# Openings of the first and third attention rearranged: barrier ahead of the gate loads, queries of the first 512 tokens between key units, normalisation on ScalarE, rows of maxima sent ahead of the last queries

## The chip, the cores and the metric

The kernel runs on one core of a Trainium2 chip as one program for the five engines of the core: PE (TensorE), DVE (VectorE), ACT (ScalarE), POOL (GpSimd) and SP (SyncE, which issues most of the DMAs). The metric is the device time of one execution in microseconds (us). Three executions of the kernel before were timed; the profile is of a fourth.

## What is computed

Four transformer layers over x, 2048 tokens of width 256. Each layer is cross attention over a context of 1601 rows of width 192, then a layer of experts (FFN); both add to x.

```
x = x + L0_xattn(layernorm(x), ctx)      # 16 heads of 16
x = x + L0_ffn(layernorm(x))             # 16 experts, top 4, and a shared one
x = x + L1_xattn(...); x = x + L1_ffn(...)   # 16 heads; 8 experts, top 2
x = x + L2_xattn(...); x = x + L2_ffn(...)   # 8 heads of 32; 8 experts, top 2
x = x + L3_xattn(...); x = x + L3_ffn(...)   # 16 heads, masked; 16 experts, top 2

def xattn(x, y):
    q = x @ Wq + bq; k = y @ Wk + bk; v = y @ Wv + bv      # split into heads
    att = softmax(q @ k.T * dh ** -0.5)                    # over the 1601 keys
    return (att @ v) @ Wo + bo
```

## The kernel before

Tokens stand in four chunks of 512 (`NQ = 4`, `Q = 512`), heads in four groups (`NG = 4`; 4 heads a group in layers 0, 1 and 3, 2 in layer 2), keys in 13 blocks of up to 128 (`NK = 13`). An attention loops over chunks (`iteration`), in a chunk over groups, in a group over the 13 key blocks: PE makes scores, ACT takes exp, PE weighs the values.

Queries and keys are held as three bf16 parts each. Such a "unit" (128 rows of queries or keys by 512 columns) goes through a pipeline with two buffers (`QK[2]`, `QP[2]`, dealt in turn by the class `Staging`; whoever fills a buffer waits until the unit before last has been split and has landed): PE projects it into PSUM, ACT copies it out twice (`copy_keys`, lines 1115 and 1116; first queries line 1150), DVE or POOL splits it into parts (`split`), SP stores it in DRAM (`store_key_parts` into `k_parts`, line 514; `store_query_parts` into `q_parts`, line 523) and loads it back stacked (`load_keys` into `k_stack`, line 457, six DMAs a group; `load_queries` into `q_stack`, lines 541, 546 and 547, seven DMAs a group). All 256 columns of keys need eight key units: units 0 to 3 hold the first two groups of heads, units 4 to 7 the other two. A chunk of queries is two units, m = 0 and 1.

The largest score of each token and head is needed before exp. It is found with 400-column "max" jobs: a matmul into one of three PSUM banks (line 2193) and a reduce on DVE (line 1458). When all of a group's jobs are through, the maxima are turned on PE, negated and split on DVE into `m_part`, and SP sends them through DRAM into the query stack (`store_max_rows`, lines 583 and 588). The scores of the group can't start before that.

Attentions 1 and 3 (`AHEAD`) have their opening hidden in the FFN ahead. Attentions 0 and 2 have an opening of their own, the prologue: the max jobs of group 0 (64 in layer 0, 32 in layer 2), the turn, and three eighths of the jobs of group 1 (24 and 12). Between them, after every second job, PE takes one item of the list `behind`: in layer 0 key units 4 to 7 (two halves each) and the 13 value blocks (lines 2109 and 2110), 21 items, and then in both layers for chunks d = 1, 2, 3 two items "turn" (the normalised chunk transposed, `turn_ahead`, line 2258) and four items "query" (`query_ahead`, line 2271). ACT copies those queries once (line 1190), and POOL makes the first part as well as the split (`split_queries`, line 874).

The very start: SP issues x's first chunk, the context and the attention weights, then x's other three chunks, the mask and the gate weights, and then comes a barrier of all five engines (`fence`); only behind it PE, ACT and DVE begin. Key units 0 to 3 run first, then DVE's statistics of x, the normalisation of chunk 0 (DVE) and of chunks 1 to 3 (POOL, line 839), and the two query units of chunk 0.

In layer 2 keys and values are projected in the FFN ahead; what is left for its opening are the statistics of x, the loads, values and queries.

In both openings SP's queue stands in one written order. In layer 0 it is: key units 0 to 3, all six loads of groups 0 and 1, the first queries, key units 4 to 7, the loads of groups 2 and 3, the rows of maxima, then the queries of chunks 1 to 3. In layer 2: the loads of group 0, the first queries, the loads of groups 1 to 3, the queries of chunks 1 to 3, then the rows of maxima.

## Time and profile before

| | |
|---|---|
| three timed runs | 3899.71, 3901.49, 3909.51 us; median 3901.49 |
| the profiled execution | 3903.35 us, span of its instructions 3901.6 us |
| busy in the span | PE 3615.8 us (93%), DVE 2534.6, ACT 1913.4, POOL 682.8 |
| granted clock of TensorE, mean | 0.964 of full speed |

Spans and starts below are microseconds from the first instruction. A busy share says that an instruction was under way, and idle time of an engine that nobody waits for costs nothing, so the two openings are read stretch by stretch, by what ended each wait.

### The profile page before, as it was taken

To read this page: it belongs to the slowest core of one execution; us is meant where nothing else is said; L and a number is where in the kernel's file an instruction comes from. 1 tells how busy PE (TensorE), PEld (TensorE's weight loads), DVE (VectorE), ACT (ScalarE), POOL (GpSimd) and SP (SyncE) were. 2 spreads that over 40 slices of the span, in tenths; PEclk is the share of its full clock that TensorE was granted. 3 is DMA by queue.
4 is the path that set the end of the run, shared out by engine and by line. 5 is a ranking of instruction groups with operands and counts; after the bars stand their busy time and mean duration, and the time that the engine had idled before them with its cause. 6 is when DMAs were issued, how large, how long until landed. Compare 5 with 4: busy or idle time off the path is not lost. (4 is left out here: it accounts for less than half of the span.)

```text
span 3901.6 us, 50396 instructions
## 1 busy us (share of the span) xinstructions
PE 3615.8 (93%) x17554; PEld 1565.4 (40%) x17555; DVE 2534.6 (65%) x5369; ACT 1913.4 (49%) x2321; POOL 682.8 (17%) x976
## 2 busy tenths in 40 slices
PE   5999999789999999987998699999789999998996
PEld 2333333355543333334665333333433333333564
DVE  4888888446678888844223555554468888885523
ACT  2677777511137777772332244445202777777111
POOL 3300001300032000013221401010403100001142
PEclk8999999889999999998999899999899999999998
DMA  6200000151000000006001500000420000001134
GB/s 133 48 19 14 18 17 7 54 100 42 21 23 27 14 19 18 10 20 242 31 30 46 118 18 18 18 18 6 87 63 21 27 13 19 18 10 43 48 124 137
DMA packets 132652, 171.33 MB, mean 44 GB/s; under 512 B 38378, under 2 KB 106588, under 8 KB 130256
## 3 DMA queue, kind: packets, MB, share of 16 engines
q1 hardware_dynamic: 122288, 142.42, 12.8%
q0 software_dynamic: 10144, 26.08, 3.4%
q8 instruction: 126, 2.06, 0.2%
q14 instruction: 94, 0.77, 0.1%
HBM read 131.27 MB, written 40.84 MB: 44 GB/s over the span
## 5 line engine op out<-in xcount | busy, mean ns | idle before, releaser
L1458 DVE TENSOR_REDUCE mx<-ps 128x1 f32<-128x400 f32 (+1 forms) x3584 | 1819.6, 567 | 500.4 <-PE ps L2193 488.6
L1206 ACT ACTIVATE probs<-ps,zero_col 128x1024 f32<-128x1024 f32 (+1 forms) x1040 | 1111.1, 1111 | 585.0 <-PE ps L2229 584.8
L2193 PE MATMUL ps<-k_stack,q_stack 97*128 97x400 bf16 (+1 forms) x3584 | 1074.5, 338 | 53.4 <-DMA q_stack<-m_parts 21.6
L2229 PE MATMUL ps<-q_stack,k_stack 100*128 100x512 bf16 (+2 forms) x3328 | 1056.3, 381 | 6.4 <-ACT probs L1206 6.4
L2243 PE MATMUL ps<-probs,v 128*32 128x512 f32 (+2 forms) x5824 | 890.8, 607 | 0.2 <-ACT probs L1206 0.2
L2193 PEld LDWEIGHTS ps<-k_stack,q_stack 97*128 97x128 bf16 x3584 | 289.8, 97 | 1049.8 <-DVE mx L1458 624.9
L1206 ACT ACTIVATE probs<-ps,mask_col 128x1024 f32<-128x1024 f32 (+1 forms) x416 | 439.5, 1110 | 158.6 <-PE ps L2229 158.6
L2229 PEld LDWEIGHTS ps<-q_stack,k_stack 100*128 100x128 bf16 (+2 forms) x3328 | 323.2, 100 | 345.0 <-ACT probs L1206 65.8
L2243 PEld LDWEIGHTS ps<-probs,v 128*32 128x32 f32 (+2 forms) x5824 | 140.0, 111 | 263.9 <-issue 248.6
L1611 DVE SCALAR_TENSOR_TENSOR x_res<-ps,comb,x_res 128x256 f32<-128x256 f32 x336 | 148.5, 480 | 87.0 <-PE ps L2485 81.9
L1274 ACT ACTIVATE h_t_s<-ps 128x512 f32<-128x512 f32 x80 | 47.8, 597 | 278.2 <-PE ps L2476 278.2
L2485 PE MATMUL ps<-w_up_s,h_t_s 128*128 128x256 f32 x640 | 166.7, 391 | 6.8 <-DVE x_res L1611 3.5
L2476 PE MATMUL ps<-xn_t,w_up_s 128*128 128x512 f32 x320 | 154.2, 605 | 18.7 <-DMA w_up_s<-in_expert 18.1
L922 POOL TENSOR_TENSOR o_t<-o_sum,recip_wide 128x512 f32<-128x512 f32 x32 | 40.8, 1274 | 711.6 <-DMA recip_wide<-row_recips 711.6
L924 POOL TENSOR_TENSOR o_sum<-o_sum,recip_wide 128x512 f32<-128x512 f32 x28 | 35.8, 1277 | 647.2 <-DMA recip_wide<-row_recips 647.2
L2566 PE MATMUL ps<-w_all,xn_t 128*128 x624 | 142.8, 382 | 3.7 <-ACT xn_t L1288 2.4
L2545 PE MATMUL ps<-w_all,xn_t 128*128 x312 | 143.3, 603 | 1.8 <-SPq L769 1.8
L2485 PEld LDWEIGHTS ps<-w_up_s,h_t_s 128*128 128x128 f32 x640 | 116.3, 192 | 60.1 <-DVE x_res L1611 26.4
L2566 PEld LDWEIGHTS ps<-w_all,xn_t 128*128 128x128 f32 x624 | 117.1, 190 | 42.0 <-issue 27.9
L1288 ACT ACTIVATE xn_t<-ps,tile_bias 128x128 f32<-128x128 f32 x312 | 84.7, 382 | 99.8 <-PE ps L2557 99.5
L2499 PE MATMUL ps<-w_up_s,xn_t 128*128 128x512 f32 x256 | 121.6, 618 | 11.0 <-DMA w_up_s<-in_we 10.4
L1318 ACT ACTIVATE silu_gate<-ps 128x320 f32<-128x320 f32 (+3 forms) x60 | 28.1, 468 | 195.5 <-PE ps L2641 152.0
(291 smaller groups left out, 2727.3 us busy)
## 6 DMA issues: line engine op xcount, KB each, us to landing
q_stack<-q_parts SPq DMA_DIRECT2D x384, 64.0 KB, 2.3
q_parts<-qk_part SPq DMA_DIRECT2D x32, 384.0 KB, 2.5
w_up<-in_up SPq DMA_DIRECT2D x17, 704.0 KB, 4.1
w_up_s<-in_expert SPq DMA_DIRECT2D x40, 256.0 KB, 2.7
k_stack<-k_parts SPq DMA_DIRECT2D x48, 200.1 KB, 8.1
k_stack<-k_parts POOLq DMA_DIRECT2D x48, 200.1 KB, 18.6
k_parts<-qk_part SPq DMA_DIRECT2D x24, 384.0 KB, 3.1
w_all<-in_up SPq DMA_DIRECT2D x8, 1024.0 KB, 15.3
```

Source lines behind the costliest of these rows:

```text
L1206: act.activation(PR[pair[0] % 4][0:r, :, :], PS[0:r, 2 * b:2 * b + 2, :], ACT.Exp, bias=mask_col[0:r, k:k + 1] if L == 3 else zero_col[0:r ...
L1288: last = act.activation(HB[:, q * P:(q + 1) * P], PS[:, 2 + q // 4, q % 4 * P:(q % 4 + 1) * P], ACT.Gelu, bias=BT[:, bass.ds(i, 1), q], sc ...
L1458: ins = dve.reduce_max(MX4[g % 2][:, u, c:c + 1], PS[:, bank, 0:CK[c]], AX.X)
L1611: dve.scalar_tensor_tensor(X[:, t, :], PS[:, b, 0:D], c, X[:, t, :], ALU.mult, ALU.add).then_inc(s_yf, 1)
L2193: last = mm(PS[:, bank, 0:CK[c]], QS[g][0:97, slot_of(j), qt * P:(qt + 1) * P], KS[0:97, (g * hpg + j) * nsub, CKO[c]:CKO[c] + CK[c]], sta ...
L2229: last = mm(PS[0:r, b + i, :], KS[0:rows, (g * hpg + jj) * nsub + sub, k * P:k * P + r], QS[g][0:rows, slot_of(jj) + sub, :], start=sub == ...
L2243: last = mm(PS[pw * jj:pw * jj + pw, 4, :], V[0:r, k, (g * hpg + jj) * pw:(g * hpg + jj) * pw + pw], PR[used[0] % 4][0:r, i, :], start=k = ...
L2476: last = mm(PS[:, n % 2, :], up[:, k, :], xnT[:, k, c * Q:(c + 1) * Q], start=k == 0, stop=k == 1)
L2485: mm(PS[:, 2 + yj[0] % 3, 0:D], HTS[n % 2][:, 0, i * P:(i + 1) * P], weight_slot(load)[1], start=True, stop=True).then_inc(s_y, 1)
L2499: last = mm(PS[:, n % 4, :], xnT[:, k, t * P:(t + 1) * P], WUS[i % 2][:, k * 512:(k + 1) * 512], start=k == 0, stop=k == 1)
L2545: last = mm(PS[:, half, :], XT1[par][:, k * P:(k + 1) * P], w1.rearrange("p a f -> p (a f)"), start=k == 0, stop=k == 1)
L2566: last = mm(PS[:, 4 + par, 0:D], HB[:, q * P:(q + 1) * P], w2.rearrange("p a f -> p (a f)"), start=q == 0, stop=q == NF // P - 1)
```

## The change

First attention (layer 0):
- The barrier stands directly behind the issue of the attention weights. The issue of x's chunks 1 to 3 comes after it on SP; the mask and the gate weights (nine DMAs) are issued by ACT ahead of its own part of the barrier.
- The units run in the order key 0, key 1, key 2, query (0,0), key 3, query (0,1) (`FIRST_UNITS`). Statistics and normalisation of chunk 0 come before them on DVE, those of chunks 1 to 3 after them.
- SP stores units 0 to 2, query (0,0) and key 3, waits for all to land, and loads queries of group 0, keys of group 0, queries of group 1, keys of group 1; only then does it store query (0,1).
- Values 4 to 12 are projected after the queries of chunks 1, 2 and 3 (`LATE_VALUES`), all through one PSUM bank, number 4.

Both openings:
- ACT instead of POOL normalises chunks 1 to 3 (`normalize_ahead`, 12 activations of 128x256, with `shift` = -mean/deviation as the bias), behind the load of the Exp table.
- ACT writes both copies of the queries of chunks 1 to 3; POOL's first copy goes.
- SP sends the rows of maxima after the queries of chunks 1 and 2 and before those of chunk 3; the keys of groups 2 and 3 are loaded last.

In layer 2 the loads of group 0 are cut in two: rows 0 and 1 ahead of the store of query (0,0), the other four behind it.

```diff
     if L == 0:
-        return keys[0:4] if part == 0 else [x for pair in zip(keys[4:8], values[0:4]) for x in pair] + values[4:]
+        return [x for pair in zip(keys[4:8], values[0:4]) for x in pair]
...
+FIRST_UNITS = ["key", "key", "key", "query", "key", "query"]
+LATE_VALUES = {1: range(4, 7), 2: range(7, 10), 3: range(10, NK)}
+
+def value_bank(L, v):
+    return 4 if L == 0 and v >= 4 else 2 + v % 2
...
             load_attention_weights(0)
+            fence(sp, fences)
             for c in range(1, NQ):
                 sp.dma_start(X[:, c * TPQ:(c + 1) * TPQ, :], x_chunks[c]).then_inc(s_in, 16)
-            sp.dma_start(mask_u8[:, 0:NK - 1], A["mask"][:, 0:P * (NK - 1)].rearrange("a (k p) -> p (a k)", p=P),
...
-            fence(sp, fences)
             load_constant_rows(0)
-            for u in range(4):
+            for u in range(3):
                 store_key_parts(u)
+            store_query_parts(0, 0)
+            store_key_parts(3)
+            wait_landed(qd)
             wait_landed(kd)
+            load_queries(0, (0, 0), 0)
             load_keys(sp, 0, 0)
+            load_queries(0, (0, 1), 1)
             load_keys(sp, 0, 1)
+            store_query_parts(0, 1)
+            wait_landed(qd)
+            load_queries(0, (0, 2), 2)
 
             def first_queries(L):
                 store_query_parts(0, 0)
+                if L == 2:
+                    load_keys(sp, 2, 0, (2, 6))
                 wait_landed(qd)
...
-                if L not in AHEAD:
-                    first_queries(L)
                 if L == 2:
-                    for g in range(1, NG):
-                        load_keys(sp, 2, g)
+                    first_queries(2)
+                    load_keys(sp, 2, 1)
                 if L == 0:
                     for u in range(4, 8):
                         store_key_parts(u)
                     wait_landed(kd)
-                    load_keys(sp, 0, 2)
-                    load_keys(sp, 0, 3)
-                    store_max_rows(L, 0)
                 if L not in AHEAD:
-                    for d in range(1, NQ):
+                    for d in range(1, NQ - 1):
                         for m in range(2):
                             store_query_parts(d, m)
-                if L == 2:
                     store_max_rows(L, 0)
+                    for m in range(2):
+                        store_query_parts(NQ - 1, m)
+                    for g in range(2, NG):
+                        load_keys(sp, L, g)
...
                 pool.wait_ge(s_qe, qe.at())
-                link(pool.tensor_copy(QP[buf][:, 0, :], QK[buf][:]))
+                if L in AHEAD:
+                    link(pool.tensor_copy(QP[buf][:, 0, :], QK[buf][:]))
                 split(QK[buf], QP[buf], Q, s_qp)
...
-                    for d in range(1, NQ):
-                        normalize_chunk(d, XNQ[d])
...
+            def normalize_ahead():
+                act.wait_ge(s_rs, rs.at())
+                for d in range(1, NQ):
+                    for i in range(TPQ):
+                        t = d * TPQ + i
+                        last = act.activation(XNQ[d][:, i, :], X[:, t, :], ACT.Identity,
+                                              bias=shift[:, t:t + 1], scale=rstd[:, t:t + 1])
+                    last.then_inc(s_xp, 1)
...
                 act.activation(warm[:], zero_col[:], ACT.Exp)
+                if L not in AHEAD:
+                    normalize_ahead()
                 if L == 0:
                     copy_projections(0, 1)
...
                 if not fresh:
-                    pe.wait_ge(s_vc, vc.at(1))
+                    pe.wait_ge(s_vc, vc.at(0 if L == 0 and v >= 4 else 1))
...
                     behind += [("query", (d, m, k)) for m in range(2) for k in range(2)]
+                    behind += [("value", n) for n in LATE_VALUES[d]] if L == 0 else []
```

On SP's queue the start of the program, from the issue of x's later chunks up to the first send of the rows of maxima, stood as follows before (the loads of mask and gates and the constant rows, which come in between, and the seven-DMA query loads are part of it).

```order
L597 DMA x_res<-in_x 128x4x256 x3
...
L514 DMA k_parts<-qk_part 128x3x512 x3
L514 DMA k_parts<-qk_part 128x3x65
L457 DMA k_stack<-k_parts 16x4x1601 x12
L523 DMA q_parts<-qk_part 128x3x512
L541 DMA q_stack<-q_parts 16x4x512 x6
...
L514 DMA k_parts<-qk_part 128x3x512 x3
L514 DMA k_parts<-qk_part 128x3x65
L457 DMA k_stack<-k_parts 16x4x1601 x12
L583 DMA m_parts<-m_part 16x4x128
L588 DMA q_stack<-m_parts 4x2048
L523 DMA q_parts<-qk_part 128x3x512 x6
```

The same queue of the changed kernel, from the key units to the last keys.

```order
L524 DMA k_parts<-qk_part 128x3x512 x3
L533 DMA q_parts<-qk_part 128x3x512
L524 DMA k_parts<-qk_part 128x3x65
L551 DMA q_stack<-q_parts 16x4x512 x6
...
L467 DMA k_stack<-k_parts 16x4x1601 x6
L551 DMA q_stack<-q_parts 16x4x512 x6
...
L467 DMA k_stack<-k_parts 16x4x1601 x6
L533 DMA q_parts<-qk_part 128x3x512
...
L533 DMA q_parts<-qk_part 128x3x512 x4
L593 DMA m_parts<-m_part 16x4x128
L598 DMA q_stack<-m_parts 4x2048
L533 DMA q_parts<-qk_part 128x3x512 x2
L467 DMA k_stack<-k_parts 16x4x1601 x12
```

The first query store moved in front of all key loads, the second one behind the loads of both groups, the maxima in front of the last two query stores, and twelve key loads behind those.

On PE, in the prologue of layer 0, the last key half (65 columns) was followed before by ten value blocks with two max jobs between each two.

```order
L2094 MATMUL ps<-ctx_b,wk 128x65
L2193 MATMUL ps<-k_stack,q_stack 128x400 x2
L2109 MATMUL ps<-wv,ctx_a 128x256
L2110 MATMUL ps<-wv,ctx_b 128x256
L2193 MATMUL ps<-k_stack,q_stack 128x401
L2193 MATMUL ps<-k_stack,q_stack 128x400
L2109 MATMUL ps<-wv,ctx_a 128x256
L2110 MATMUL ps<-wv,ctx_b 128x256
```

In the changed kernel one value block (number 3) follows it and then the first transposes of chunk 1.

```order
L2153 MATMUL ps<-ctx_b,wk 128x65
L2255 MATMUL ps<-k_stack,q_stack 128x400 x2
L2168 MATMUL ps<-wv,ctx_a 128x256
L2169 MATMUL ps<-wv,ctx_b 128x256
L2255 MATMUL ps<-k_stack,q_stack 128x401
L2255 MATMUL ps<-k_stack,q_stack 128x400
L2320 MATMUL ps<-ident,probs 128x128 x4
```

The transposes, which wait for ACT's copy of key unit 7 (`pe.wait_ge(s_kc, kc.at())` in `turn_ahead`), moved from item 22 of `behind` to item 13.

On SP's queue in the opening of layer 2, behind the last loads of the FFN, there stood before:

```order
L503 DMA k_stack<-const_rows 1x16x1601 x4
L457 DMA k_stack<-k_parts 32x2x1601 x6
L523 DMA q_parts<-qk_part 128x3x512
L546 DMA q_stack<-q_parts 32x2x512 x6
...
L523 DMA q_parts<-qk_part 128x3x512
L546 DMA q_stack<-q_parts 32x2x512 x6
...
L457 DMA k_stack<-k_parts 32x2x1601 x18
L523 DMA q_parts<-qk_part 128x3x512 x6
L583 DMA m_parts<-m_part 8x4x128
L588 DMA q_stack<-m_parts 4x2x512
```

and in the changed kernel:

```order
L513 DMA k_stack<-const_rows 1x16x1601 x4
L467 DMA k_stack<-k_parts 32x2x1601 x2
L533 DMA q_parts<-qk_part 128x3x512
L467 DMA k_stack<-k_parts 32x2x1601 x4
...
L467 DMA k_stack<-k_parts 32x2x1601 x6
L533 DMA q_parts<-qk_part 128x3x512 x4
L593 DMA m_parts<-m_part 8x4x128
L598 DMA q_stack<-m_parts 4x2x512
L533 DMA q_parts<-qk_part 128x3x512 x2
L467 DMA k_stack<-k_parts 32x2x1601 x12
```

Of the six query stores ahead of the rows of maxima two moved behind them, and with them the keys of groups 2 and 3.

## Rows read from the trace of the kernel before

**Rows 1.** The page, section 1: busy us, share, instructions of each engine.

```profile
PE 3615.8 (93%) x17554; PEld 1565.4 (40%) x17555; DVE 2534.6 (65%) x5369; ACT 1913.4 (49%) x2321; POOL 682.8 (17%) x976
```

**Rows 2.** Windows: stretch, length, busy PE, PEld, DVE, ACT, POOL, clock, DMA share, GB/s.

```profile
28.50:64.20 35.70, 7.97 (x16) 3.95 (x16) 16.29 (x54) 6.84 (x14) 15.44 (x12) 0.60 0.73 123
64.20:73.50 9.30, 9.27 (x18) 4.56 (x19) 4.23 (x8) 1.53 (x4) 2.91 (x3) 0.50 0.40 123
82.95:123.80 40.85, 35.92 (x150) 19.39 (x150) 34.25 (x71) 11.70 (x32) 16.46 (x21) 0.97 0.63 108
...
2174.50:2202.00 27.50, 23.94 (x93) 10.95 (x93) 22.61 (x49) 6.71 (x12) 14.78 (x15) 1.00 0.82 185
2202.00:2223.50 21.50, 0.02 (x1) 0.06 (x2) 0.96 (x2) 1.37 (x2) 18.29 (x23) 0.53 0.30 101
```

**Rows 3.** Timeline of SP's queue, first opening: start, length, instruction.

```profile
7.16 0.35 SPq L494 DMA_DIRECT2D bo<-in_bo  x1
...
10.72 1.35 SPq L598 DMA_DIRECT2D mask_u<-in_mask  x1
...
26.50 7.79 SPq L514 DMA_DIRECT2D k_parts<-qk_part  x4
37.22 5.49 SPq L457 DMA_DIRECT2D k_stack<-k_parts  x12
...
52.37 0.38 SPq L523 DMA_DIRECT2D q_parts<-qk_part  x1
...
59.40 2.65 SPq L541 DMA_DIRECT2D q_stack<-q_parts  x6
...
73.50 10.91 SPq L514 DMA_DIRECT2D k_parts<-qk_part  x4
```

**Rows 4.** Timeline of DVE and ACT, first opening; in brackets the idle time before.

```profile
19.46 1.41 DVE L1434 BATCH_NORM_STATS2 stat<-x_res 128x6 f32<-128x256 f32 x4 [19.33 <-SPq L436]
30.28 0.60 ACT L1115 ACTIVATE qk<-ps 128x512 f32<-128x512 f32 x1 [2.93 <-DMA k_parts<-qk_part]
...
82.59 0.23 ACT L1115 ACTIVATE qk<-ps 128x65 f32<-128x65 f32 x1 [2.36 <-DMA k_parts<-qk_part]
```

**Rows 5.** Windows, for DMA: the start, and two stretches full of key loads.

```profile
2.00:28.00 26.00, 8.52 (x15) 3.70 (x15) 4.02 (x8) 2.74 (x6) 12.35 (x11) 1.00 0.92 183
38.00:58.00 20.00, 7.97 (x16) 3.95 (x16) 9.20 (x34) 5.41 (x10) 15.44 (x12) 0.59 1.03 137
2182.60:2202.00 19.40, 16.56 (x64) 7.20 (x62) 16.42 (x37) 4.02 (x7) 6.68 (x8) 1.00 0.99 207
```

**Rows 6.** Prices: ACT's timeline in the second FFN; groups by line, 64.2 to 123.8.

```profile
2109.41 2.17 ACT L1288 ACTIVATE xn_t<-ps,tile_bias 128x128 f32<-128x128 f32 x8
...
L1127 ACT ACTIVATE v<-ps 128x128 f32<-128x128 f32 (+1 forms) x26 | 5.8, 275 | 8.5 <-PE ps L2110 8.2
```

**Rows 7.** Waits of PE, 2140 to 2300: line, released by, us, times, longest.

```profile
PE ps L2193 <- DMA q_stack<-m_parts: 21.6, 1, 21.6
```

**Rows 8.** Timeline of SP's queue, opening of layer 2.

```profile
2161.53 0.52 SPq L523 DMA_DIRECT2D q_parts<-qk_part  x1
2169.80 2.65 SPq L546 DMA_DIRECT2D q_stack<-q_parts  x6
...
2219.57 0.39 SPq L583 DMA_DIRECT2D m_parts<-m_part  x1
```

**Rows 9.** Timeline of ACT, DVE and POOL, opening of layer 2; window of a slow stretch.

```profile
2173.72 1.28 ACT L1173 ACT_TABLE_LOAD   x1
...
2176.47 1.09 ACT L1184 ACTIVATE xn_t<-ps 128x512 f32<-128x512 f32 x2 [1.25 <-PE ps L2258]
...
2196.90 0.28 DVE L1474 TENSOR_TENSOR m_part<-m_rest,m_part 8x128 bf16<-8x128 f32 x1
...
2204.31 0.61 POOL L874 CAST qk_part<-qk 128x512 bf16<-128x512 f32 x1 [14.58 <-DMA q_parts<-qk_part]
...
2169.00:2172.60 3.60, 3.60 (x10) 2.58 (x9) 0.00 (x0) 1.32 (x6) 3.60 (x4) 0.53 0.27 84
```

More of the change, by code:

```diff
@@ L203, in build @@
         rstd = sb("rstd", [P, NT])
+        shift = sb("shift", [P, NT])
         WQ = sb("wq", [P, 2, D])
@@ L892, in _ @@
             clear_values(0)
-            for u in range(4):
-                staged.take("key")
-                kc.step()
-                kp.step()
+            for kind in FIRST_UNITS:
+                staged.take(kind)
+            kc.step(4)
+            kp.step(4)
             for L in range(4):
@@ L1540, in _ @@
                             staged.take("key")
+                        for m in range(6):
+                            staged.take("query")
                     tab_ready.step(2)
```

152 lines of the change are left out of this document (94 added, 58 removed).

## Prediction

> **What bounds the kernel now.** I read the page's busy shares first: PE works 93% of the span [rows 1], so only stretches in which PE stands still, or runs at the low clock, have time to give. I then cut both openings into windows [rows 2] and asked the waits who ended each gap. From 28.5 to 64.2 PE is busy 8.0 of 35.7 us: the first max job starts at 64.2. From 2202.0 to 2223.5 it is not busy at all, and the wait is one of 21.6 us for the rows of maxima [rows 7]. Between 64.2 and 123.8 (scores begin) PE is nearly full, 9.3 us of it at half clock (0.50).
>
> First opening. The barrier opens at 19.46 (DVE's first row, 19.33 us idle [rows 4]). Key stores go out from 26.50, and ACT's copy of unit 2 waits until 30.28 for the landing of unit 0 [rows 3, 4]. All four have landed at 37.22, where SP issues the twelve key loads; these fill the DMA engines from 38 to 58 (share 1.03 at 137 GB/s, [rows 5]). The first query unit, stored at 52.37, lands behind them, 7.0 us later, at 59.40 [rows 3]; 4.8 us more for its load give 64.2. What is late is the query, and ahead of it the key bytes.
>
> Third opening. The `m_part` of group 0 is ready at 2197.18 [rows 9], but SP sends it at 2219.57, behind six query stores [rows 8], the last of which ends POOL's chain of four splits from 2204.31 on. So the 21.5 us are the order of a queue.
>
> **The change part by part: third opening.** The maxima go out after four query stores. I follow the units with ACT's two copies (1.4 us), POOL's split without its first copy (four units in 15.3 us from 2204.31 to 2219.57 [rows 8, 9] are 3.8 each; less that copy and its gap, 0.7, gives 3.1) and 2.7 us to land (an estimate: 2219.57 to the wait's end at 2223.5 is 3.9 for a store and a load in a row). The fourth unit is split near 2198.5. The maxima are ready at 2197.2 plus what the prologue is late, are sent at about 2201, and are there at 2205.
>
> Late by how much? ACT normalises behind its table load, from 2175.2 (2173.72 + 1.28 + the warm one). Before, POOL had done it, unseen, and ACT copied the first turned chunk at 2176.47 [rows 9]. A 128x256 activation isn't in the trace. Bounds: 0.27 us (2.17 / 8 at 128x128, [rows 6]) and 0.55 (1.09 / 2 at 128x512, [rows 9]); I take 0.37. Twelve are 4.5 us (3.3 to 6.5), and the copy of chunk 1 stands behind all twelve: 2179.7 instead of 2176.5, 3.2 us late (2.0 to 5.2). PE waits for it. The 2 + 4 split of the first key loads lets query (0,0) land earlier than its 8.3 us (2161.53 to 2169.80 [rows 8]), but PE's value blocks end at 2173.2 whatever SP does (ACT's table load at 2173.72 follows their last copy), so this gives 1.3 us at most. The late key loads of groups 2 and 3 are 2.4 MB, 11.6 us at 207 GB/s [rows 5]; issued near 2206 they have group 2 landed by 2215 and group 3 by 2221. The first max job on group 2 stands behind 20 others in the first group of scores, 10 us at 0.48 us a DVE instruction (34.25 / 71 [rows 2]) or more: hidden, with at most 1 us to wait. Sum: 21.5 + 1.3 - 3.2 - 1.6 (chunk 3's copy waiting its turn behind a landing, and a restart at lower clock after the new wait: at 2169.0 to 2172.6 a wait of 3 us was followed by a clock of 0.53 [rows 9]) = **18.0 us saved** (14 to 20).
>
> **First opening.** SP's last issue ahead of the barrier ends at 7.51 [rows 3]; the nine small loads took SP from 10.72 to just before 19.46, 8.7 us [rows 3, 4]. On ACT, from about 1.0 on, they can take as long or less: the barrier stands between 7.7 and 9.7. I take 9.7, 9.8 us earlier. That is not what the path gets: the same DMAs must still run ahead of the key stores. Share 0.92 over 26 us [rows 5] is 23.9 us of all engines' work; packed, it ends at 25.9 instead of 28. With a landing time of 2 to 3 us unit 0 has landed near 27.5 (25.5 to 28.5), 2.8 us earlier. Then: key 2 copied 28.7, query (0,0) 30.1, split by DVE 32.8, key 3 after key 2's landing (33.7), stored 35.1, landed 38.0. SP loads queries (3.2 us for seven DMAs) and keys 0; 1.2 MB at 137 GB/s are 8.8 us, at the 10 us per six loads of 38 to 58 a little more: first max job at 51 (46 to 55) instead of 64.2, 13.2 us saved. One group of keys rather than two stands ahead of it.
>
> What is late next. Query (0,1) is stored behind the keys of group 1, so it lands with them, about 14 us after the first job (10 for the keys, the rest queries and landing). Key unit 5 shares its buffer: its copy waits for that. SP then loads seven query DMAs (3.2 us) before it stores unit 4, which before was stored 9.3 us after the first job (73.50 against 64.2 [rows 3]) and now 18. Copy 1.2, split 3.1, store and landing 3.3: unit 7 is copied about 22.5 to 23 us after the first job. Before, this was 18.4 (82.59 [rows 4]) and did not matter, as the transposes were item 22. Now they are item 13, reached 18.75 us after the first job (82.95, where the 13th item began): PE stands 4.0 us (3 to 6), and a clock of 0.5 behind it, as at 2169, costs 1.5. Values 4 to 12 through one bank: six times PE waits for a copy of two activations of 275 ns [rows 6] less what runs meanwhile, 0.4 each, 2.5 us (0 to 3, nothing if DVE's reduces set the pace). The old end, where POOL's chain held the last queries back, gives 1.0. POOL and ACT swap the normalisation here too; ACT is done near 50, in time. The keys of groups 2 and 3, 2.4 MB at 137 GB/s, 17.5 us, are issued about 10 us before the scores begin, and group 2 is needed behind 40 max jobs, 19 us or more after: hidden. Sum: 13.2 - 4.0 - 1.5 - 2.5 + 1.0 = **6.2 us saved** (0 to 15).
>
> **Sum.** 24.2 us. From the profiled execution, 3903.35 (span 3901.6): 3879.2. The median of the runs is 1.9 lower, so 3877.3; I give 3877. A difference under 0.3% (12 us) is about what a measurement of this kernel can't tell from none.
>
> A rule of the Trainium skill, beside these rows. DMA: Bandwidth & Descriptors, section "Issuing engines are not separate DMA queues", says that DMAs issued by SP, ACT and POOL run on the same 16 engines and interleave, so that a second issuing engine saves issue time alone. Without it the barrier's 9.8 us would all be gained and the time would be 3870; with it the packed engines allow 2.8 us, as in the sum. The trace of before has no DMA from ACT and cannot show it.
>
> **The rivals.**
> - The first opening keeps its gain (0.20). The stores land earlier and unit 7's chain keeps up. For it: the start has gaps, and `behind` advances slowly at half clock. Against: SP's written order, which puts 1.2 MB ahead of query (0,1). 15 + 19 = 34 us: 3867.
> - The first opening gives all back (0.17): the mask's and gates' packets hold up the context and the weights, the first job comes at 55, the stall is 6 us, the clock stays low longer. 1 + 15 = 16 us: 3886.
> - The wait of the third opening is only moved (0.06): the maxima are sent after the fourth split, and if landings take 5 us instead of 2.7, as behind full queues, the wait is still 9 us. 24 - 9 = 15 us: 3887.
> - Slower (0.03): the clock. If the new small waits of the prologues kept PE at the low level through all 40.9 us from item 13 on, and the 27.5 us in layer 2, now at 0.97 and 1.00 [rows 2], PE's 36 and 24 busy us would need up to twice that: 60 us against 24 saved, 3937. It turns slower once 24 us of full-clock work run at half. Against: the small waits between 82.95 and 123.8 (PE idle 4.9 us in all) left the clock at 0.97.
> - No change to be told (0.04): both the second and third together, and loads that reach into the scores. 3893.
>
> **The numbers.** The forecast, 3871 to 3883, has 0.50; from 3862 (the first rival with every bound) to 3889 is 0.8 and more. Faster by over 0.3%: 0.93; within: 0.04; slower: 0.03.
>
> **What would show it.** Right: PE's first max job at 46 to 55; a wait of PE on ACT's key copy 18 to 19 us behind it; scores of layer 0 near 117; in layer 2 PE waiting for ACT's transposed chunk about 3 us, no wait over 3 us for the rows of maxima, scores of group 0 some 18 us earlier relative to the end of the FFN. Wrong: a first job after 55, a wait for keys inside the first groups, normalisations above 0.55 us, or a clock of 0.5 in the prologues beyond their first 10 us.

## The result and the profile after

The changed kernel takes 3886.35 us (median of 8 runs, 3882.83 to 3889.02) against 3901.39 us for the kernel before (8 runs, 3896.61 to 3909.51): ratio 0.9960, 95% interval 0.9949 to 0.9971, 15.0 us faster. Its profiled execution took 3888.28 us with a span of 3886.5. A second set of five runs gave 3887.85 and 0.9965 (0.9952 to 0.9977).

The page of the changed kernel, busy shares and DMA queues. It answers to [rows 1]; q10, the queue of ScalarE's DMAs, is new.

```profile
PE 3628.4 (93%) x17554; PEld 1570.2 (40%) x17555; DVE 2536.1 (65%) x5373; ACT 1931.6 (50%) x2358; POOL 645.1 (17%) x940
...
q10 hardware_dynamic: 3008, 0.15, 0.1%
```

Shares say nothing here; the waits of PE do. Those of the two openings, out of the list for the whole span of the changed kernel (line waiting, what it waited for, us in total, times, longest):

```profile
...
PE ps L2255 <- DMA k_stack<-k_parts: 27.7, 1, 27.7
...
PE ps L2151 <- DMA wk<-in_bk: 13.6, 1, 13.6
...
PE ps L2320 <- ACT qk_part L1136: 5.8, 1, 5.8
...
PE ps L2333 <- ACT xn_t L1228: 4.1, 5, 1.6
...
PE ps L2320 <- ACT probs L1185: 3.0, 1, 3.0
```

The 21.6 us for the rows of maxima [rows 7] are gone. New are 5.8 us ahead of the first turned chunk of layer 0, and 3.0 us in layer 2 for ScalarE's normalising. PE does not begin at the barrier any more (19.46 [rows 4]) but at 13.6, when the last load that its first matmul needs has landed.

Stretches of the two openings, changed kernel (columns as in [rows 2]):

```profile
28.50:54.76 26.26, 0.00 (x0) 0.03 (x1) 13.10 (x45) 11.64 (x24) 0.00 (x0) 0.54 0.60 110
64.20:76.45 12.25, 6.25 (x28) 3.44 (x26) 6.90 (x14) 3.14 (x12) 3.47 (x4) 0.94 0.43 128
76.45:85.00 8.55, 8.04 (x20) 4.11 (x21) 3.17 (x6) 1.62 (x5) 3.19 (x6) 0.50 0.18 52
85.00:122.70 37.70, 32.87 (x132) 16.88 (x130) 30.20 (x63) 13.35 (x34) 23.36 (x27) 0.95 0.30 80
2168.01:2180.00 11.99, 7.43 (x20) 3.90 (x21) 4.22 (x8) 8.31 (x16) 0.00 (x0) 0.61 0.68 166
2180.00:2206.03 26.03, 21.82 (x76) 9.04 (x75) 20.89 (x43) 9.76 (x16) 19.78 (x22) 0.89 0.29 94
```

The first max job stands at 54.76, 9.5 us earlier than 64.2, but the scores of layer 0 begin at 122.70, only 1.1 us earlier than 123.8: behind the stall PE has 8 us at half clock (0.50). In layer 2 the scores begin 38.0 us behind the first max job (2168.01 to 2206.03) instead of 49.5 (2174.56 to 2224.10). This distance leaves out that before, PE waited 1.3 us for a load ahead of that first job; now it waits 0.5 us there, for ScalarE. Counted from ScalarE's first square root of layer 2's statistics (2144.21 before, 2138.45 now), the scores begin after 67.6 us instead of 79.9.

SP's queue in the changed kernel, first opening; it answers to [rows 3].

```profile
20.41 12.64 SPq L524 DMA_DIRECT2D k_parts<-qk_part  x3
34.48 0.36 SPq L533 DMA_DIRECT2D q_parts<-qk_part  x1
37.01 0.36 SPq L524 DMA_DIRECT2D k_parts<-qk_part  x1
39.34 2.69 SPq L551 DMA_DIRECT2D q_stack<-q_parts  x6
...
48.96 3.77 SPq L467 DMA_DIRECT2D k_stack<-k_parts  x6
52.78 0.49 SPq L533 DMA_DIRECT2D q_parts<-qk_part  x1
66.51 2.65 SPq L551 DMA_DIRECT2D q_stack<-q_parts  x6
...
69.75 10.57 SPq L524 DMA_DIRECT2D k_parts<-qk_part  x4
```

Query (0,1) is stored at 52.78; SP's next issue, which waits for its landing, is at 66.51. ScalarE waits for the same landing, as unit 5 shares the buffer, and unit 7 comes at 76:

```profile
29.67 0.60 ACT L1135 ACTIVATE qk<-ps 128x512 f32<-128x512 f32 x1 [6.94 <-DMA k_parts<-qk_part]
...
66.60 0.60 ACT L1135 ACTIVATE qk<-ps 128x512 f32<-128x512 f32 x1 [5.99 <-DMA q_parts<-qk_part]
...
74.74 0.60 ACT L1135 ACTIVATE qk<-ps 128x512 f32<-128x512 f32 x1 [6.71 <-DMA k_parts<-qk_part]
...
76.02 0.26 ACT L1135 ACTIVATE qk<-ps 128x65 f32<-128x65 f32 x1
```

ScalarE in layer 2, changed kernel: table load, normalising, and only then the first turned chunk (before, that copy stood 1.5 us behind the end of the table load [rows 9], now 6.0).

```profile
2167.97 1.28 ACT L1215 ACT_TABLE_LOAD   x1
...
2169.38 6.00 ACT L1185 ACTIVATE probs<-x_res,shift,rstd 128x256 f32<-128x256 f32 x12
2175.28 1.05 ACT L1228 ACTIVATE xn_t<-ps 128x512 f32<-128x512 f32 x2
```

Twelve in 6.0 us are 0.50 each. SP sends the maxima at 2199.51, ahead of the last two query stores at 2201.13 (before: 2219.57, behind all six [rows 8]).

### The profile page after: what moved, and what is told of

Read it like the earlier page. It is cut to its first block and busy times, and to the rows that moved or that the text cites. A ratio compares the mean times of both kernels' runs of the same rounds, so it can differ in the third digit from the quotient of the medians.

```text
span 3886.5 us, 50411 instructions
## 1 busy us (share of the span) xinstructions
PE 3628.4 (93%) x17554; PEld 1570.2 (40%) x17555; DVE 2536.1 (65%) x5373; ACT 1931.6 (50%) x2358; POOL 645.1 (17%) x940
## 5 line engine op out<-in xcount | busy, mean ns | idle before, releaser
L2555 PEld LDWEIGHTS ps<-w_up_s,h_t_s 128*128 128x128 f32 x640 | 115.3, 191 | 59.7 <-DVE x_res L1670 26.3
## 6 DMA issues: line engine op xcount, KB each, us to landing
w_all<-in_up SPq DMA_DIRECT2D x8, 1024.0 KB, 11.5
```

The costliest lines, as they stand in the source:

```text
L2555: mm(PS[:, 2 + yj[0] % 3, 0:D], HTS[n % 2][:, 0, i * P:(i + 1) * P], weight_slot(load)[1], start=True, stop=True).then_inc(s_y, 1)
```

## The experiments

Times of one kernel scatter by 5 us and more, so verdicts go by intervals, and mechanisms by landmarks of the profiled executions, each read from the first row of its kind. Outside the openings, executions differ by what PE waits for the experts' weights: 28.5 us in that of the kernel before, 23.1 in the changed one, 31.2 in e8's and 21.9 in e9's. The profiled run of e8 (3888.78) lies 15 us above its median: 9 us are these waits, and 6 arose in the third attention, which takes 587.3 us there, 581.2 in e5 and e9. The distances within an opening don't contain the waits for weights. For layer 2 there are two distances. The one from the square root is that of the expectations below; it holds what happens ahead of the first max job as well, and differs by 2.5 us between the two executions of the changed kernel, the other one by 0.8.

| kernel | median us | ratio to before (95%) | first max job | wait ahead of the first turn | scores L0 begin | L2: first max job to scores | L2: first square root to scores |
|---|---|---|---|---|---|---|---|
| before | 3901.39 | 1 | 64.23 | 0 | 123.82 | 49.54 | 79.9 |
| changed | 3886.35 | 0.9960 (0.9949 to 0.9971) | 54.76 | 5.79 | 122.70 | 38.02 | 67.6 |
| changed again | 3887.85 | 0.9965 (0.9952 to 0.9977) | 54.28 | 5.33 | 121.97 | 37.23 | 65.1 |
| e1 | 3884.83 | 0.9955 (0.9941 to 0.9968) | 64.75 | 0 | 124.32 | 30.72 | 60.3 |
| e2 | 3903.33 | 1.0006 (0.9996 to 1.0016) | 63.84 | 0 | 124.56 | 47.62 | 78.1 |
| e3 | 3884.67 | 0.9953 (0.9940 to 0.9967) | 54.48 | 0 | 115.41 | 38.87 | 66.8 |
| e4 | 3888.20 | 0.9959 (0.9945 to 0.9972) | 54.17 | 5.14 | 122.01 | 33.62 | 61.6 |
| e5 | 3875.01 | 0.9935 (0.9922 to 0.9948) | 54.78 | 0.79 | 114.26 | 32.48 | 60.4 |
| e6 | 3883.63 | 0.9953 (0.9940 to 0.9966) | 55.63 | 3.19 | 121.29 | 37.33 | 65.2 |
| e7 | 3877.77 | 0.9930 (0.9917 to 0.9943) | 54.73 | 0 | 118.05 | 30.80 | 60.4 |
| e8 | 3873.62 | 0.9928 (0.9913 to 0.9942) | 54.25 | 0 | 115.06 | 31.77 | 62.5 |
| e9 | 3874.80 | 0.9935 (0.9920 to 0.9950) | 56.02 | 0 | 114.94 | 31.78 | 59.7 |
| e10 | 3880.86 | 0.9943 (0.9930 to 0.9956) | 55.04 | 0 | 115.98 | 39.15 | 68.7 |
| e11 | 3876.09 | 0.9929 (0.9912 to 0.9946) | 56.76 | 0 | 117.84 | 31.89 | 61.4 |

My theory after the result: the third opening's gain is SP's order less what ScalarE's normalising costs; the first opening's gain is the order of queries and keys, given back by the store of query (0,1). Rivals: the barrier carries part of the gain; unit 7 is late whatever the store does; ScalarE's second copies, not its normalising, are the cost.

**e1_order_layer2.** Of the change, only SP's order in layer 2, with the split of the first key loads.

```diff
                 store_query_parts(0, 0)
+                if L == 2:
+                    load_keys(sp, 2, 0, (2, 6))
                 wait_landed(qd)
...
                 if L == 2:
+                    for d in range(1, NQ - 1):
+                        for m in range(2):
+                            store_query_parts(d, m)
                     store_max_rows(L, 0)
+                    for m in range(2):
+                        store_query_parts(NQ - 1, m)
+                    for g in range(2, NG):
+                        load_keys(sp, L, g)
```

> The kernel before with SP's order of the third attention alone: key loads of group 0 in 2 + 4, the rows of maxima behind the fourth query store, keys of groups 2 and 3 last. GpSimd normalises and copies as before, the first attention is untouched. My theory (the 21.5 us are the order of a queue): the wait for the rows of maxima falls from 21.6 us to under 5, and the scores of layer 2 begin 18 to 20 us earlier relative to the opening's start, more than the 12.3 us that the changed kernel shows, since no normalisation by ScalarE delays its prologue. Time 3882 to 3884. Rival A (the gain of 12.3 us in the changed kernel needed ScalarE's help, GpSimd's chain being late): 9 to 12 us, 3890. Rival B (the wait moves to keys of groups 2 and 3, loaded late): under 5 us, and a wait of TensorE for keys within the first scores of layer 2.

The first max job to the scores takes 30.7 us instead of 49.5: 18.8 us gained, against 11.5 to 12.3 by the whole change. From the square root it is 19.6 us, against 12.3 to 14.8. SP's queue of e1:

```profile
2183.20 11.51 SPq L524 DMA_DIRECT2D q_parts<-qk_part  x4
2195.05 0.29 SPq L584 DMA_DIRECT2D m_parts<-m_part  x1
2197.04 0.26 SPq L589 DMA_DIRECT2D q_stack<-m_parts  x1
2198.05 4.08 SPq L524 DMA_DIRECT2D q_parts<-qk_part  x2
2202.17 5.84 SPq L458 DMA_DIRECT2D k_stack<-k_parts  x12
```

So a re-ordering of one queue, with no work moved, gives what the whole change gives: the intervals are 0.9941 to 0.9968 and 0.9949 to 0.9971. No wait for the late keys shows. Rivals A and B fall.

**e2_barrier_alone.** The kernel before with the barrier behind the weights and the small loads on ScalarE.

> The kernel before with the barrier directly behind the attention weights and the nine small loads issued by ScalarE; all else as before. Theory (what sets the landing of the first key stores is the work of the DMA engines, not the barrier): the barrier opens near 9.3 instead of 19.46, but ScalarE's first wait for a landing ends at most 1 to 2 us earlier than 30.28 and the first max job comes at 62 to 64 instead of 64.2; time 3900 to 3902, no change that can be told. Rival (the barrier's delay passes through the chain): first max job near 55, 3892. Second rival (the small loads on a second queue hold up the context and the weights): the first max job 1 to 3 us later, 3903.

```profile
9.10 1.28 ACT L1161 ACT_TABLE_LOAD   x1 [9.10 <-issue]
...
29.73 0.60 ACT L1115 ACTIVATE qk<-ps 128x512 f32<-128x512 f32 x1 [8.93 <-DMA k_parts<-qk_part]
```

The barrier opens 10 us earlier, and the landing that ScalarE waits for comes 0.55 us earlier (30.28 [rows 4]). The DMA engines are full from 2 to 28:

```profile
2.00:28.00 26.00, 8.48 (x16) 3.83 (x16) 5.03 (x10) 3.66 (x6) 12.19 (x11) 0.95 0.99 206
```

Share 0.99 at 206 GB/s, against 0.92 at 183 [rows 5]. The first key store goes out at 20.13 instead of 26.50, 6.4 us earlier, for those 0.55 us. By the rule of the Trainium skill quoted in the prediction (DMA: Bandwidth & Descriptors, "Issuing engines are not separate DMA queues") a second issuing engine saves issue time alone; the trace agrees, with 0.4 us at the first max job for 10 us at the barrier.

**e3_query_store_ahead.** The changed kernel with one line moved.

```diff
             load_keys(sp, 0, 0)
+            store_query_parts(0, 1)
             load_queries(0, (0, 1), 1)
             load_keys(sp, 0, 1)
-            store_query_parts(0, 1)
             wait_landed(qd)
```

> The changed kernel with one line moved: query (0,1) is stored ahead of the loads of queries (0,1) and keys of group 1, right behind the key loads of group 0. Theory (the 5.8 us stall at the first turn and the 8 us of low clock behind it are the landing of this store behind 1.2 MB of loads): ScalarE copies unit 5 by about 58 instead of 66.6, unit 7 before TensorE arrives, stall under 1 us, clock high from there; the scores of layer 0 begin 7 to 10 us earlier, time 3877 to 3880. Rival (the chain through two staging buffers is late anyway, and each of units 4 to 7 waits for a store to land behind loads): the stall shrinks to 2 to 4 us, the clock still falls, gain 2 to 4 us, 3883. Rival on the other side: the store, waited for by SP before its next loads, delays the keys of group 1, and the first max jobs wait: 0 us or slower by 2.

```profile
45.70 0.43 SPq L533 DMA_DIRECT2D q_parts<-qk_part  x1
...
55.38 2.65 SPq L551 DMA_DIRECT2D q_stack<-q_parts  x6
...
63.78 10.20 SPq L524 DMA_DIRECT2D k_parts<-qk_part  x4
```

The store has landed at 55.4 instead of 66.5, unit 7 is copied at 71.96, ahead of the first turn at 72.77, and PE doesn't wait:

```profile
71.96 0.23 ACT L1135 ACTIVATE qk<-ps 128x65 f32<-128x65 f32 x1 [1.90 <-DMA k_parts<-qk_part]
```

```profile
72.77 0.60 PE L2320 MATMUL ps<-ident,probs 128*128 128x128 f32 x4
```

The next window row shows the clock that goes with it (0.50 in the changed kernel's row):

```profile
73.50:85.00 11.50, 10.46 (x44) 5.73 (x44) 8.74 (x18) 4.74 (x12) 5.62 (x7) 1.00 0.24 74
```

The scores begin 7.3 us earlier than in the changed kernel: 5.8 of wait and the low clock behind it, less some 2 us by which PE reached its first turn later than in the changed kernel (more on that at e11). So the first opening's gain was there and was given back by one line. The time expected, 3877 to 3880, did not come: 3884.67. The end of the first attention is 6.2 us earlier (722.9 against 729.1), but the stretch from there to layer 2 takes 4.2 us longer in e3's profiled execution, which no edit of e3 touches. The medians don't part e3 from the changed kernel; the landmark does, beyond the 0.7 us by which the changed kernel's two executions differ there.

**e4_pool_normalises_l2** and **e10_one_copy_act_normalises** part ScalarE's two new tasks in layer 2. e4 is the changed kernel with

```diff
                 else:
+                    for d in range(1, NQ) if L == 2 else []:
+                        normalize_chunk(d, XNQ[d])
...
-                if L not in AHEAD:
+                if L == 0:
                     normalize_ahead()
```

e10 is e3 with ScalarE's single copy and GpSimd's first part back in layer 2:

```diff
-                if L in AHEAD:
+                if L > 0:
                     link(pool.tensor_copy(QP[buf][:, 0, :], QK[buf][:]))
...
+                        if L == 2:
+                            buf, before = staged.take("query")
+                            act.wait_ge(before[0], before[1])
+                            act.activation(QK[buf][:], PS[:, 2 + m, :], ACT.Identity, bias=BQS[:, m:m + 1],
+                                           scale=scale).then_inc(s_qe, 1)
+                            continue
```

> The changed kernel, but in the third attention GpSimd normalises chunks 1 to 3 as before and ScalarE does not; the first attention is as in the changed kernel. Theory (ScalarE's twelve activations of 0.5 us delay the turned chunks, and with them the prologue and the rows of maxima): TensorE's waits of 3.0 and 1.6 us in the opening and the low clock behind them go, scores of layer 2 begin 5 to 6 us earlier, time 3880 to 3881. Rival A (GpSimd's chain of four splits is the path, and it began at the same place in both kernels): nothing, 3886. Rival B (GpSimd's normalising now overlaps the query splits that come sooner): rows of maxima are waited for, 2 to 4 us slower.

> The kernel of e3 with one thing of the third attention as before: ScalarE makes one copy of each query unit and GpSimd the first part, but ScalarE still normalises all twelve tiles in a row. It parts the two costs that ScalarE's new work has in the third opening, where the changed kernel's scores begin 65 to 67.6 us behind the first rstd and those of e1 and e5 60.3. Theory (the normalising is most of it, since the copy of turned chunk 1 stands behind it): scores at 64 to 66, time 3880 to 3883. Rival (the wait of ScalarE's second copy for the landing of the store before it in the same buffer is most of it): scores at 61 to 62, 3877.

Without ScalarE's normalising, the distance to the scores falls from 38.0 and 37.2 to 33.6, by 4.0 us on the mean (from the square root from 67.6 and 65.1 to 61.6, by 4.8). GpSimd takes 14.5 us for it and starts its first split at 2179.8, 3.3 us behind the unit's copy. With the single copy but ScalarE normalising it stays at 39.2 (e3, same but for the copies: 38.9); from the square root it is 68.7, above the 64 to 66 expected and far from the rival's 61 to 62. So the normalising is the cost, and theory holds on that. e4's own median shows no gain against the changed kernel (3888.20): 4 us are within the scatter. In e4 the second copies have a price of their own, since ScalarE may write the staging buffer only when its last store has landed:

```profile
2185.66 0.69 ACT L1236 ACTIVATE qk<-ps,bq_scaled 128x512 f32<-128x512 f32 x1 [5.25 <-DMA q_parts<-qk_part]
```

PE stands behind it, and the turned chunks come 10.4 us apart (2179.32 and 2189.73) instead of 7.5 in e1. This wait is a reason why the gain, 4.0 to 4.8 us, stayed under the 5 to 6 foreseen; e5, with a single copy and GpSimd's normalising, is 1.1 us better (32.5), which alone is no more than scatter.

**e5_combined.** e3, and layer 2's engines as before (GpSimd normalises and makes the first copy).

> The changed kernel with the store of query (0,1) ahead of the loads of group 1 (as e3), and in the third attention the engines of the kernel before: GpSimd normalises chunks 1 to 3 and makes the first copy of the query units, ScalarE makes one copy; SP's order stays that of the change. Theory (the gains of e3 in the first opening, 7.9 us to the end of the first attention, and of e1 in the third, 17.6 us from the opening to the end of its attention, are independent): the first attention ends near 723, the third is 583.5 us long from its opening on, span 3901.6 - 7.9 - 17.6 = 3876, time 3876 to 3878. Rival (the third opening's last 3 us, which e1 has over the kernel with GpSimd's normalising alone, came from the state in which the first opening leaves the rest): 586.5 and 3880.

3875.01 us, ratio 0.9935 (0.9922 to 0.9948): faster than the changed kernel of the same set (0.9965, 0.9952 to 0.9977; the intervals do not meet). The square root behind the first attention stands at 721.8 against 729.1 in the changed kernel, and that behind the third is 581.2 us from the opening's against 590.8. The two gains add up, 7.3 us in the first attention and 9.6 in the third.

**e6_small_loads_on_sp.** The changed kernel with the small loads back on SP, ahead of the barrier.

> The changed kernel with the nine small loads issued by SP ahead of the barrier, as in the kernel before; all else as changed. Theory (the key stores' landing is set by the DMA engines' work; of the 9.4 us by which the first max job comes earlier, the barrier gives at most 1 us and the order of queries and keys the rest): barrier at 19 to 20, first max job at 54.5 to 56, the stall at the first turn as in the changed kernel; time 3886 to 3888, no change against the changed kernel. Rival (the barrier gives half or more): first max job at 59 or later, 3890 to 3892.

```profile
16.01 2.07 PE L2151 MATMUL ps<-ctx_a,wk 128*128 128x512 f32 x2 [16.01 <-SPq L445]
...
55.63 0.83 PE L2255 MATMUL ps<-k_stack,q_stack 97*128 97x401 bf16 x2 [24.59 <-DMA k_stack<-k_parts]
```

The barrier opens at 16.0 instead of 9.3, the first max job comes 0.9 to 1.3 us later, and the scores 0.7 to 1.4 us earlier. The stall was expected to stay and is 3.2 us instead of 5.8: the first job is later, and unit 7's copy comes at 74.8 instead of 76.0. The time is 3883.63 against 3887.85 beside it, if anything faster. Of the 9.5 us of the first max job the barrier gives one. The rest comes from what else was re-ordered there, the units, the loads and the statistics, which no run takes apart; that one group of keys instead of two stands ahead of the query is what the queue shows.

**e7_values_ahead.** e5 with values 4 to 12 of layer 0 ahead of the turned chunks, through two banks.

```diff
-        return [x for pair in zip(keys[4:8], values[0:4]) for x in pair]
+        return [x for pair in zip(keys[4:8], values[0:4]) for x in pair] + values[4:]
...
-LATE_VALUES = {1: range(4, 7), 2: range(7, 10), 3: range(10, NK)}
+LATE_VALUES = {1: (), 2: (), 3: ()}
...
-    return 4 if L == 0 and v >= 4 else 2 + v % 2
+    return 2 + v % 2
```

> The kernel of e5 with the nine values 4 to 12 of the first attention in the place and the banks that they had in the kernel before: all ahead of the turned chunks, through two banks. Theory (one bank costs TensorE 0.45 us at each of six values, and nothing stalls at the first turn any more once the query is stored ahead): the six waits of 0.19 us on ScalarE's value copies go, scores of layer 0 begin 2 to 3 us earlier than in e5, 3874. Rival A (VectorE's reduces set the pace of the prologue, 29 of every 32 us busy): within 1 us of e5. Rival B (GpSimd's chain of query splits, which then starts 8 us later behind the values, becomes the end of the prologue): the rows of maxima wait behind query stores, scores 2 to 6 us later than in e5.

The six waits of 0.19 us go, as foreseen, and the scores begin 3.8 us later (118.05), though both medians and intervals overlap. Rival B named a time like this, and the rows of maxima were indeed sent 2.2 us after they were ready (101.27), behind the fourth query store; but PE never waited for them. Neither theory nor a rival had named the reason, which VectorE's rows of e7 show. These are the steps that split the maxima:

```profile
98.22 0.70 DVE L1542 TENSOR_TENSOR m_rest<-m_neg,m_part 16x128 f32<-16x128 f32 x1
98.96 1.13 DVE L1543 CAST m_part<-m_rest 16x128 bf16<-16x128 f32 x1
100.13 1.14 DVE L1544 TENSOR_TENSOR m_part<-m_rest,m_part 16x128 bf16<-16x128 f32 x1
```

In e5, where GpSimd has nothing to do from 96 to 102, the last two:

```profile
99.44 0.21 DVE L1543 CAST m_part<-m_rest 16x128 bf16<-16x128 f32 x1
99.69 0.28 DVE L1544 TENSOR_TENSOR m_part<-m_rest,m_part 16x128 bf16<-16x128 f32 x1
```

With the queries 11 us later in the program, GpSimd splits queries from 96.96 to 103 just where VectorE splits the maxima. Four steps take 3.3 us instead of 1.0, VectorE's reduces stop, PE waits 2.6 us for them, and behind this wait it is at the low clock again (0.91 us for two max jobs that take 0.51 at full clock):

```profile
101.81 0.91 PE L2263 MATMUL ps<-k_stack,q_stack 97*128 97x400 bf16 x2 [2.63 <-DVE mx L1528]
```

The single bank costs 0.45 us at each of six values by the starts of PE's rows (an estimate, 2.7 us in all), but taking it away gained nothing. What can be seen to cost time here is what runs beside the split of the maxima; a run that changes that alone was not made.

**c_after_again.**

> The changed kernel itself once more, beside the kernels of this set, as the measure of what two runs of one kernel differ by: 3884 to 3888, and a profiled span within 3 us of 3886.5, with the same first max job (54.8), stall at the first turn (5.8) and normalisations (0.50 us each). If a landmark moves by more than 1 us within an opening, verdicts on differences of that size fall.

First max job 0.5 us earlier, scores of layer 0 0.7 us, distance in layer 2 0.8 us: differences under 1 us within an opening say nothing, nor do those under 2.5 us from the square root (67.6 and 65.1).

**e8_shared_normalising.** e5 with GpSimd normalising chunk 1 alone in layer 2, ScalarE chunks 2 and 3 in its gaps.

```diff
+                    for d in range(1, 2) if L == 2 else []:
+                        normalize_chunk(d, XNQ[d])
...
                         act.activation(xnT[:, half, d * Q:(d + 1) * Q], PS[:, half, :], ACT.Copy).then_inc(s_xtc, 1)
+                    if L == 2 and d < NQ - 1:
+                        normalize_ahead(d + 1, d + 2)
```

> The kernel of e5, but in the third attention GpSimd normalises chunk 1 alone, and ScalarE normalises chunks 2 and 3, four activations each, behind its copies of turned chunk 1 and of turned chunk 2. Theory (in e5 GpSimd's 14.5 us of normalising hold its first query split back until 2179.4, 2.4 us after the unit is there, while ScalarE has gaps of 2.4 us that take four activations of 0.5 us): the first split comes 2 us earlier, the rows of maxima and the scores of layer 2 at most 2 us earlier relative to the opening; 3873 to 3875. Rival (VectorE's reduces set the pace of the prologue): scores within 0.5 us of e5's 60.3 us behind the first rstd of layer 2. Rival on the other side (the activations delay ScalarE's query copies): scores 1 to 2 us later.

31.8 us instead of 32.5, and 3873.62: not to be told from e5. From the square root, the measure of the expectation, it is 62.5 us against 60.4, which would be the second rival; but e9 and e11, the same code in layer 2, show 59.7 and 61.4, and e8's 2 us arose ahead of the first max job (30.8 us behind the square root, 27.9 in e5 and e9), before any activation that was moved. So there is no gain and no loss to be told. From the first max job, all kernels whose chunk 1 is GpSimd's and whose copies are single (e1, e5, e7, e8, e9 and e11) lie between 30.7 and 32.5 us, although GpSimd is busy 31.1 us of them in e5 and 24.0 in e8: it does not pace that prologue. That VectorE's reduces do, as the first rival says, is argued and not shown: VectorE is busy 25.5 and 26.3 us of them, and PE 25.4 and 25.9.

**e9_shared_small_on_sp** and **e11_values_cleared_late.** e9 is e8 with e6's edit; e11 is e9 with GpSimd's memset moved:

```diff
             fence(pool, fences)
-            clear_values(0)
...
                 pool.wait_ge(s_rs, rs.at())
+                if L == 0:
+                    clear_values(0)
```

> The kernel of e8 with the nine small loads issued by SP ahead of the barrier, as in e6. Theory (the barrier gives at most 1 us): first max job 1 us later than in e8, scores of layer 0 within 1.5 us of e8's, same time. Rival (with the query stored ahead, the later start of the keys lets unit 7's chain keep up and nothing is lost, and the context and weights come sooner without a second queue): 1 to 2 us faster than e8.

> The kernel of e9 with GpSimd's clearing of the values (a memset of 128x6656, 5.65 us) moved from just behind the barrier to behind the statistics of all chunks, near 47, where GpSimd is idle. In the changed kernel VectorE's small scaling of the variances takes 3.77 us instead of 0.17 and ends at 15.01, where that memset ends too (9.35 + 5.65 = 15.00); in e6 the same at 21.68 and 21.67. Theory (VectorE is held by GpSimd's memset, and this holds ScalarE's first key copies behind the square root): the operation takes 0.2 us, the square root comes 3.6 us earlier at 18.1, the first key store 1.5 to 3 us earlier than e9's, the first max job 1 to 3 us earlier (53 to 55 instead of 56.0), time 3872 to 3874. Rival A (what the operation waits for is something else of the start): it still takes over 3 us. Rival B (it takes 0.2 us, but the landing of unit 0 is set by the DMA engines' queue): first wait for a landing ends within 0.5 us of e9's, first max job at 55.5 to 56, no gain.

e9 is e8 within the scatter: first max job 1.8 us later, scores within 0.2; the 1 to 2 us of its rival don't show. e11 settles what the DMA engines do to the first opening. VectorE's operation takes 0.17 us in it, and the square root and the first key store come 3 us earlier (23.08 instead of 26.04), but the landing of unit 0 doesn't. ScalarE in e9, then in e11:

```profile
31.44 0.60 ACT L1137 ACTIVATE qk<-ps 128x512 f32<-128x512 f32 x1 [4.94 <-DMA k_parts<-qk_part]
```

```profile
31.63 0.60 ACT L1138 ACTIVATE qk<-ps 128x512 f32<-128x512 f32 x1 [7.23 <-DMA k_parts<-qk_part]
```

The engine waits 2.3 us longer for the same moment: rival B. Stored 3 us earlier here, or 6.4 us earlier in e2, the unit lands within 0.6 us of the same moment. That packets ahead of it hold it is the reading that fits: from 18 to 31 the DMA engines are 0.90 busy in e9 and 0.96 in e11. e11's scores come 2.9 us later than e9's: 0.7 is the first max job, the rest the clock. The ten us behind that job, e9 and then e11:

```profile
56.00:66.00 10.00, 9.98 (x31) 5.37 (x32) 6.64 (x13) 3.06 (x8) 3.44 (x4) 0.79 1.05 188
```

```profile
56.00:66.00 10.00, 9.24 (x20) 4.65 (x21) 4.23 (x8) 1.53 (x4) 2.91 (x3) 0.53 1.07 204
```

PE issues 31 matmuls in one and 20 in the other, and its first turn comes 16.3 and 18.45 us behind the first job. Both values recur: 16 to 17 in the changed kernel, e5 and e9, 18.2 to 18.5 in e3, e8, e10 and e11. Equal code shows both (e3 and e5 have the same first opening), so what decides between them stays open.

The fastest versions are e5, e7, e8, e9 and e11, ratios 0.9928 to 0.9935, which these runs do not part. They share the order of the change in both openings, query (0,1) stored ahead of group 1, and layer 2's normalising off ScalarE's path, on GpSimd or in ScalarE's gaps.

## Why the prediction came out as it did

The time, 3886.35, lies in the range (3862 to 3889) and on the side foretold, but 9 us above the value and outside the likeliest case's own 3871 to 3883. Both openings gave less: forecast 6.2 and 18.0 us; when the scores begin, 1.1 to 1.9 and, from the square root, 12.3 to 14.8 were measured. Of the 15.1 us between the profiled spans of the two kernels 1.7 stand at the end of the first attention, 4.1 arose from there to layer 2's square root, 10.2 in the third attention, and 0.9 were lost behind it. The 4.1 us are no effect of the change that can be told: that stretch, the same code everywhere but for the last key loads in it, takes 1407.5 to 1416.1 us in the fourteen profiled executions. Nor do these rows say why some 2 us of the third opening's gain are gone by the end of its attention (in e1 too, 19.6 and 17.5). That the time fell in the range is thus in part luck: what the two attentions gave, 11.9 us (13.3 in the second execution), would alone have made 3888 to 3889.5, the range's upper edge.

- **Barrier at 9.7**: 9.32. **Unit 0 landed at 27.5** (25.5 to 28.5): 29.67, outside the bounds. I had let packed engines finish 2.1 us sooner; e2 shows share 0.99 and 0.55 us gained, and e11 that an earlier store doesn't help. The engines were full, as I had said, and still did not finish the work ahead of the landing sooner.
- **First max job at 51** (46 to 55): 54.76, a miss of 3.8 us. 1.3 us are the start of the loads (39.34, not 38.0: unit 0's landing and, behind it, unit 3, stored at 37.0 and not 35.1), and 2.4 us the loads: 15.4 us from SP's first query load to the job, where I had 13. The stretch in the changed kernel:

```profile
39.34:54.76 15.42, 0.00 (x0) 0.03 (x1) 7.99 (x35) 7.59 (x15) 0.00 (x0) 0.50 0.83 129
```

Share 0.83 at 129 GB/s: I had taken the rate of engines that were full throughout, and the first loads, issued one by one, did not fill them. That this is the reason was not tried by a run.
- **Stall of 4.0 us** (3 to 6): 5.8. Unit 7's copy came 21.5 us behind the first job, near the 22.5 forecast; the error was on the other side, as PE reached the first turn after 15.9 us, not 18.75: the clock rose sooner, one of the two courses that e9 and e11 show. The mechanism, store (0,1) behind group 1's keys, is shown by e3.
- **Clock 1.5 us**: PE's 8.04 busy us at 0.50 would be 4 at full clock, so by this estimate it cost 4. I took the cost from one wait of 3 us; a wait of 5.8 was followed by 8.5 us at half clock.
- **Values 2.5 us**: 2.7 estimated from the rows, but e7, which takes the single bank away, gains nothing.
- **Order of SP in layer 2**: no wait for the maxima. The 21.5 + 1.3 - 1.6 us, 21.2, measured 19.6 (e1, from the square root).
- **ScalarE's normalising 0.37 us each, first turned chunk 3.2 us late** (2.0 to 5.2): 0.50 each, within the bounds of 0.27 and 0.55, and nearer the upper; the copy of the turned chunk stands 6.0 us behind the table load instead of 1.5, 4.6 us late. PE stood 3.0 and 1.6 us, with a clock of 0.61 over the 12 us that hold these waits; PE's 7.4 busy us there cost about 3 us by the clock (an estimate). The whole is the changed kernel against e1: 6.5 to 7.3 us from the first max job, 4.8 to 7.3 from the square root. The sum had 3.2, and for the clock no more than a part of its 1.6. So the mechanism was right, and both sizes, the activation and the clock behind the wait, were too small.
- **Keys of groups 2 and 3 hidden**: so they were, in every kernel.

The second rival gave the right number (1 + 15 = 16 us: 3886) with half the right reason. The first job at 55, a stall of 6 and the clock are what happened; that the mask's and gates' packets were to blame is not borne out by e6, where SP issues them ahead of the barrier and the first job stands at 55.6 all the same. The first rival, keys keeping up, is what e3 makes true. Slower did not come near: the low clock lasted 8.5 us behind the stall and some 9 us behind the wait in layer 2.

## What to carry to other kernels

Ask of each transfer in a queue who needs it soonest, and not only of the one that is waited for: the gain of this change lay in two orders in SP's queue, and a third misplacement in the same queue, one store behind 1.2 MB of keys, took most of one of them back. Price a new wait of TensorE with the low clock behind it: here waits of 5.8 us, and of 3.0 and 1.6 us, cost an estimated 4 and 3 us more by the clock. And ask what the DMA engines still have to move when a barrier opens: here it opened 10 us earlier ahead of full engines, and 0.4 us were gained. A distance between two marks also needs a second one: the one from the first max job left out a wait ahead of it.

## What the runs showed of the hardware

VectorE's small operations are held by GpSimd. In the changed kernel, VectorE and then GpSimd behind the barrier:

```profile
11.24 3.77 DVE L1435 TENSOR_SCALAR mv<-mv 128x4 f32<-128x4 f32 x1
```

```profile
9.35 5.65 POOL L887 MEMSET v<- 128x6656 f32 x1 [2.03 <-ACTq L445]
```

They end together: 11.24 + 3.77 = 15.01, 9.35 + 5.65 = 15.00; in e6 at 21.68 and 21.67. With the memset elsewhere the operation takes 0.17 us (e11). The Trainium skill has the rule (SBUF — State Buffer, section "Who interferes with whom"): VectorE and GpSimd share a pair of ports, a cast or tensor_scalar of VectorE in a two-port mode and an instruction of GpSimd exclude each other whole, a tensor_tensor with two inputs from SBUF contends with GpSimd's reads, and a tensor_reduce does not contend. The traces agree as far as they go: beside GpSimd's split a cast takes 1.13 us instead of 0.21 and a tensor_tensor 0.70 and 1.14 instead of 0.28 (e7 and e5), and the reduces, which read PSUM, keep their 0.5 to 0.6 us each. In which mode the casts ran no trace shows.

A moved store on a full machine does not move its landing: 6.4 us earlier at the store gave 0.55 us (e2), 3 us earlier gave none (e11).
